# An attention layer on one core: the wait for the row of maxima is put in front of the two products that read it, instead of in front of the whole first score block

## The reference

```python
q = conv1x1(Wq)          # [B, 12, 64, 1024], likewise k and v
scores = jnp.einsum('bhdn,bhdm->bhnm', q, k) * scale
attn = jax.nn.softmax(scores, axis=-1)
out = jnp.einsum('bhnm,bhdm->bhdn', attn, v)
out = out.reshape(B, C, H, W)
return x + jnp.einsum('oc,bchw->bohw', Wp, out)
```

## Time and profile before

| | |
|---|---|
| median of 3 runs | 3404.21 us (3401.08 to 3405.39) |
| the profiled execution's own time | 3401.64 us |
| its span in the profile | 3399.8 us |
| PE busy | 3321.5 us, 98% of the span |
| POOL busy | 1833.6 us, 54% |
| DVE busy | 1784.2 us, 52% |
| ACT busy | 1089.1 us, 32% |
| score blocks (L746) | 4608 matmuls of products 0 to 2, 1536 of product 3 |

### The profile page before, as it was taken

One profiled execution on the slowest core, in us unless ns is written; L12 is line 12 of the kernel. 1 busy time (PEld: TensorE's weight loads), 2 busy tenths in 40 slices (PEclk: granted clock), 3 DMA queues, 4 the chain that ended last, 5 costly groups with the idle time before them and its releaser, 6 DMA issues.

```text
span 3399.8 us, 51561 instructions
## 1 busy us (share of the span) xinstructions
PE 3321.5 (98%) x18272; PEld 2252.7 (66%) x18272; DVE 1784.2 (52%) x2417; ACT 1089.1 (32%) x1944; POOL 1833.6 (54%) x789
## 2 busy tenths in 40 slices
PE   7999999999999979999999999999999999999999
PEld 6888888888888854445555555555555555555557
DVE  5333323233233147776666666666666666666652
ACT  3111111111111114444444444444444444444441
POOL 2000000000000029998888888888888888888883
PEclk9999999999999979999999999999999999999999
DMA  6232433423243342334434434344344344343434
GB/s 234 103 137 105 146 130 123 147 99 137 101 145 109 112 152 81 118 122 144 152 118 151 149 132 162 119 162 156 124 155 150 121 143 154 125 162 125 156 106 167
DMA packets 221700, 461.90 MB, mean 136 GB/s; under 512 B 22961, under 2 KB 73009, under 8 KB 220209
## 3 DMA queue, kind: packets, MB, share of 16 engines
q1 hardware_dynamic: 221488, 459.16, 38.7%
HBM read 259.06 MB, written 199.62 MB: 135 GB/s over the span
## 4 chain that ended last, share of the span: by engine, by line
PE 56%; DMA 3%; issue 2%; DVE 1%; SPq 1%; POOL 1%; ACT 0%; ACTq 0%; POOLq 0%; DVEq 0%
PE psum L746 20%; PE psum L759 19%; PE psum L769 10%; PE psum L731 7%; PE psum L828 1%; DMA recip_rows<-compact 1%; DMA top<-turned 1%; DVE half_max L902 1%; POOL sums L702 0%; ACT p_all L862 0%; SPq L573 0%; SPq L582 0%; DMA k<-k_parts 0%; DVE flipped L912 0%; DVE compact L941 0%
## 5 line engine op out<-in xcount | busy, mean ns | idle before, releaser
L702 POOL TENSOR_TENSOR sums<-sums,p_all 128x1024 f32<-128x1024 f32 x576 | 1352.8, 2392 | 0.0
L902 DVE TENSOR_REDUCE half_max<-psum 128x2 f32<-128x1024 f32 x768 | 939.1, 1224 | 514.7 <-PE psum L731 496.7
L862 ACT ACTIVATE p_all<-psum 128x512 f32<-128x512 f32 x1536 | 792.9, 601 | 925.0 <-PE psum L746 920.8
L759 PE MATMUL psum<-p_all,v 128*64 128x512 f32 x3072 | 743.4, 605 | 0.0
L746 PE MATMUL psum<-q,k 64*128 64x512 f32 x4608 | 672.6, 397 | 20.6 <-DMA top<-turned 17.8
L710 POOL TENSOR_TENSOR wp<-sums,wp 128x1536 fp32r<-128x1536 f32 x1 | 3.4, 3449 | 1176.9 <-ACT wp L888 1176.9
L746 PEld LDWEIGHTS psum<-q,k 64*128 64x128 f32 x4608 | 427.1, 185 | 136.7 <-ACT p_all L862 34.3
L240 PE MATMUL psum<-xn_hi,w_hi 128*128 128x512 f32 x1128 | 439.6, 390 | 0.6 <-DVE stage L380 0.6
L240 PE MATMUL psum<-xn_hi,w_lo 128*128 128x512 f32 x1128 | 439.0, 389 | 0.0
L240 PE MATMUL psum<-xn_lo,w_hi 128*128 128x512 f32 x1128 | 439.0, 389 | 0.0
L290 ACT CAST stage<-psum 128x512 fp32r<-128x512 f32 x192 | 112.7, 588 | 961.6 <-PE psum L240 951.5
(11 more groups left out here) (78 smaller groups left out, 2569.2 us busy)
## 6 DMA issues: line engine op xcount, KB each, us to landing
q_parts<-stage SPq DMA_DIRECT2D x192, 256.0 KB, 2.2
k_parts<-stage SPq DMA_DIRECT2D x192, 256.0 KB, 2.3
q<-q_parts SPq DMA_DIRECT2D x48, 1024.0 KB, 5.0
k<-k_parts SPq DMA_DIRECT2D x48, 1024.0 KB, 7.4
a<-o_parts SPq DMA_DIRECT2D x84, 512.0 KB, 7.6
v_rows<-stage SPq DMA_DIRECT2D x128, 192.0 KB, 2.1
v<-v_rows SPq DMA_DIRECT2D x48, 512.0 KB, 4.7
recip_all<-recip_rows SPq DMA_DIRECT2D x96, 256.0 KB, 3.9
```

The source lines that it names most:

```text
L702: pool.tensor_tensor(sums[:, m % 2, i, :], first, p_all[:, i, n, :], ALU.add).then_inc(added, 1)
L759: mm = pe.matmul(heads[part, h, :], v[:, e, t, part], p_all[:, i, (m * MT + t) % EXPS, cols], start=(t == 0), stop=(t == MT - 1))
L862: act.activation(p_all[:, i, (m * MT + t) % EXPS, h * BANK:(h + 1) * BANK], psum[:, SCORE_BANKS[2 * h + i], :], ACT.Exp, scale=SCALE).then ...
L902: dve.tensor_reduce(half_max[:, :, t, h], of, AX.X, ALU.max, negate=True).then_inc(max_done, 1)
```

## The change

The wait for `top_in` moves from the front of the first block of a pass to the front of its product 3. It is still one wait in each pass, for the same value, on the same engine; the six matmuls of products 0 to 2 now stand in front of it. Nothing else differs: no DMA, no other wait and no operation is added, removed or moved.

```diff
             def scores_by_key(p, m, t, h):
                 e = m % SLOTS
-                if t == 0 and h == 0:
-                    pe.wait_ge(top_in, 32 * (p + 1))
                 wait(pe, exp_done, (p * MT + t) * 4 + 2 * h - 2)
...
                 for c in range(4):
+                    if t == 0 and h == 0 and c == 3:
+                        pe.wait_ge(top_in, 32 * (p + 1))
                     for i, part in enumerate(half_of):
```

## The result

The changed kernel took 3409.56 us (median of 22 runs, 3406.46 to 3411.81), the kernel before 3403.79 us (22 runs beside it). The ratio is 1.0017, 95% interval 1.0010 to 1.0023: slower by 5.8 us, where 9.8 us less was forecast. The profiled execution has a span of 3408.3 us, 8.5 more than that of before.

The account below looks back on a forecast made before the run. PE, busy 98% of the span, was taken as the bound. Gains of 5.7 us (passes 9 to 47), 3.5 (passes 0 to 8) and 0.6 (clock) made 9.8 off 3404.2, rounded to 3394.5 us, range 3390.0 to 3399.0.

Parts of the forecast that it names:

- What the change does at one wait: PE at the maxima wait: six matmuls run ahead of it, no instruction added or removed, 0.75 us gained per long wait.
- four rivals: Alternative outcomes: all early waits count (0.12), the row lands later (0.13), slower by a bubble (0.05), nothing changes (0.04).
- Rival 3: Moved wait empties PE's pipe before product 3 in every pass; at 0.3 us each, 3409 us; chance 0.05.
- Passes 9 to 47: Maxima waits in these passes: POOL has room, so PE keeps its gain; 5.7 us less.
- rival 2: In passes with projection loads, DMA traffic delays the maxima row and gives the gain back; about 3400 us; chance 0.13.
- Passes 0 to 8, with the clock: Early maxima waits give 3.5 us, limited by POOL, plus 0.6 us from the clock falling less.
- POOL as the limit of passes 3 to 6: POOL, never idle there, makes a faster PE meet late sums; only 0.1 us gained of a possible 3.0.
- rival 1: All nine early waits count, POOL does not hold PE; 3.0 us more, clock 2.0 more; 3389.4 us; chance 0.12.
- The clock behind the long waits: Shorter waits in passes 7 and 8 might keep PE's clock up; 0.6 us of a possible 2.6.

Follow-up runs that it names:

- pad11: Changed kernel plus one wait already over before the first block of each of passes 1 to 11; 3391.94 us against 3403.32 for the kernel before.
- looponly: Kernel before with the wait moved to product 3 only in the loop's passes (12 to 41); 3397.21 us against 3403.32.
- before_m1: Kernel before with the wait one matmul later in pass 11 alone, one separate wait instruction fewer ahead of the loop; 3425.30 us against 3402.91.
- only3to6: Kernel before with the wait moved in passes 3 to 6 alone, an already-over wait in its old place; 3401.02 us against 3401.90.
- second: Kernel before with the wait in front of the first block's second matmul in all passes; 3418.59 us against 3403.32, ratio 1.0047.
- pad10: Changed kernel plus 10 already-over waits in passes 1 to 11; 3412.41 us against 3401.90 for the kernel before, ratio 1.0031.
- pad256: Changed kernel plus 256 already-over waits in passes 1 to 11; 3406.70 us against 3401.90 for the kernel before, ratio 1.0012.

## Why the prediction was wrong

**The step that failed** is the first sentence of "What the change does at one wait": "It adds and removes no instruction". By the source that is so, and no operation was added or removed. In PE's list it removes 17, since of two waits in front of one matmul one takes an instruction of its own, and two waits at two matmuls don't. The chain from there to the time: 11 of them ahead of the loop, the loop 11 instructions ahead of a block's start, a second stall of 1.5 to 2.2 us at each of four turns (7.0 us), 1.0 us more of busy time behind each, the clock down for 6.8 us in two of them (2.7 us more each), 16.5 us in sum. None of the four rivals had this. Rival 3 had the right sign and the wrong place: it looked for a bubble at product 3, and the 0.70 us there have not changed. That its 3409 us is also the time measured is chance. The profile of before did show four waits "PE psum L731 <- issue" of 5.3 us at the turns; I set them aside as untouched by the change, and so never asked what decides their length.

**The gain at the wait came, though its parts are less well met than the sum.** pad11, the change without its shift, is its measure: 11.4 us less in the medians and 3399.8 - 3390.1 = 9.7 in the two traces (3.3 up to pass 9, 5.0 from there to pass 42, 1.4 behind), against a forecast of 9.8.

- Passes 9 to 47: forecast 5.7 us, measured 6.4 in pad11's trace. looponly, which has most of it, gives 6.1 us in the median and 4.7 in the trace for passes 9 to 41, where 4.2 was forecast. In pad11 PE reaches pass 42 1458.86 us after pass 9, before 1463.89: 5.0 us less. DMA traffic did not push the row of maxima back (rival 2).
- Passes 0 to 8, with the clock: forecast 3.5 + 0.6 = 4.1. In pad11 pass 9's first block starts at 1605.63 instead of 1608.91: 3.3 us. But looponly and before_m1 have the waits of passes 0 to 8 where the kernel before has them, and start pass 9 at 1607.52 and 1607.80. The mean of these three traces is 1608.1, that of the eight traces with the wait moved in all of these passes 1606.2 (the changed kernel 1606.82): 1.9 us. So this term was probably put too high, by up to a factor of two.
- POOL as the limit of passes 3 to 6 (against rival 1): shown by only3to6. In the changed kernel POOL's first addition of pass 2 came at 1335.09 instead of 1336.77, 1.7 us sooner where 1.9 was forecast.
- The clock behind the long waits: forecast 0.6 us gained. The forecast took pass 7's wait of 2.91 us and the fall of the clock behind it for the kernel's, but they seem to be that one execution's. In looponly and before_m1, with pass 7's wait in its old place, the idle time was 1.46 and 1.17 us, and the clock stayed up, as it did in the changed kernel behind 1.11 us. looponly's first block of pass 7, and PE behind it (busy, granted clock, DMA share, GB/s):

```profile
1517.68 0.97 PE L748 MATMUL psum<-q,k 64*128 64x512 f32 x6 [1.46 <-DMA top<-turned]
...
1518.50:1522.00 3.50, 3.39 (x30) 1.00 1.02 410
```

  In pass 8 the idle time was 3.43 us (2.6 was forecast) and the clock fell, in the changed kernel for 6.8 us instead of 3.4, in pad11 for 3.4. No run shows a gain by the clock that is the change's.
- The loss is not in the moved wait. With pad11, looponly and second the two effects separate: some 11 us gained at the wait, some 17 lost at the turns.

What stays open: why the clock fell behind the second stall in two turns of the changed kernel and not in the other two, and what makes a turn's own stall 1.1 us in one place and 1.7 in another. How much of the 9.8 us each term gives can't be told better than to 1 or 2 us from one trace of each kernel.

## What to carry to other kernels

A change to an engine's list that comes before a loop also moves the loop, and a loop that begins close to the end of a block of 256 instructions waits for two fetches instead of one at each turn: here 4 to 6 us more a turn. When a small edit moves the time in a way its waits do not explain, look for waits that "issue" ended at the loop's turns, count the executed instructions, and measure the edit with two different numbers of empty waits ahead of the loop, say 27 and 128 as here, before judging it; one number alone could itself bring the loop to a bad place. Two waits in front of one instruction cost an instruction more, so moving a wait changes the length of the list, even where nothing is added.

## What the runs showed of the hardware

- One separate semaphore wait more or fewer ahead of a loop of PE, where the loop begins with a block, changed the kernel by 20 us or more: pad10 3412.41 and pad11 3391.94 us (ratios 1.0031 and 0.9969), before_m1 3425.30 and the kernel before 3402.91 us.
- The effect repeats after 256 instructions and not after 128. With 30 or more instructions left behind the branch it is all but gone; with 11 left it is a second stall of 1.4 to 2.2 us; with one left a single stall of 4.2 to 5.2 us.
- Adding 128 waits that are over to the written-out passes cost nothing that shows (ratio 0.9969 to the kernel before, as in pad11).
- Behind each branch back in the attention loop at least two blocks are fetched, the second 3.0 to 4.1 us behind the first, in well and badly placed kernels alike. A loop of this length that does not begin with a block fetches one block more a turn (127 packets against 123).
- The clock fell to 1.2 GHz for 3.4 or 6.8 us at turns with a second or a double stall, in two of four in the changed kernel and in second, in all four in pad256, pad10 and before_m1, and at none of the turns with one stall of 1.1 to 1.7 us.
- A loop that is short enough is not fetched again. The first phase's loop over the images has some 730 matmuls with their weight loads a turn; from 310 to 1070 us the transfers of the kernel before list no instruction queue at all, only this line:

```profile
q1 hardware_dynamic: 68480, 94.98, 35.3%
```

The attention loop has 262 matmuls a pass in six passes, 3144 instructions with their loads, and pays at each turn.
